# Two edits to a graph and expert network: the bases load into runs of 30 partitions, and slots are looked up by one-hot products inside the routed stage

## The chip, the cores and the metric

The kernel runs on one core of a Trainium2 chip. Its time is the device time of one execution in microseconds (us); of several executions the median is given. A profile shows one execution: its span runs from the first instruction to the last.

## The reference, cut to what matters

A network over 10,000 nodes of width 512: a relational graph network, a feed-forward layer with 16 experts, a four-layer graph network and a quantized feed-forward layer. Two pieces of it are touched. The relation weights are sums over 30 bases:

```python
w = jnp.einsum('rb,bio->rio', att, basis)        # basis (30, 512, 512), att (2, 30), for each of two layers
```

and in the expert layer each expert takes the 625 tokens with the largest probability for it:

```python
flat_probs = probs.transpose(2, 0, 1).reshape(En, T)      # (16, 10000)
scores, tok_idx = jax.lax.top_k(flat_probs, cap)          # cap = 625
toks = xf[tok_idx]
h = jax.nn.gelu(jnp.einsum('ecd,edh->ech', toks, w1) + b1[:, None, :])
y = jnp.einsum('ech,ehd->ecd', h, w2) + b2[:, None, :]
y = y * scores[..., None]
routed = jnp.zeros_like(xf).at[tok_idx.reshape(-1)].add(y.reshape(-1, Dn))
```

A token may be taken by several experts, so the sums of different experts meet in the same rows. Within one expert all tokens differ.

## The kernel before, in words

The program is a row of stages (`core.phase`), each with its own semaphores and ended by a barrier of all engines. In a stage every engine has its own instruction list, written out by hand: `pipeline` and `static_pipeline` take a list of (lag, step) and issue, turn by turn, step(turn - lag) in the order of the list. `pipeline` rolls the middle turns into a loop, `static_pipeline` writes all out.

`front_phase` sorts the edges, normalizes the rows of x and combines the bases. The 512 input rows of a basis matrix are taken in blocks of 64 (`SIDE`); a product on PE (line 558) has contraction 120 = 30 bases x 4 rows (`BASIS_ROWS`), and its stationary operand `spread` holds the att values in a staircase, so that 16 products give 64 rows of both relations. SP loads half a block as four transfers, one for each `quarter` (line 353), into `ba_t`: partition 4b + quarter holds basis b. One transfer fills 30 partitions, each with 8 rows of 2 KB, and the 30 source places lie 1 MiB apart. `spread` is filled in the same order (line 342). Four halves fit into the ring; SP waits for `cb` before it reuses one. Between the bases stand the loads of x (line 358), and stores of `normed` and of the combined blocks go out on ACT's queue.

The expert layer: `tokens_phase` writes the probabilities. `select_phase` finds each expert's 625 largest and leaves in DRAM `table`, for each expert 80 rows (`NB`), one for each block of 125 tokens (`BLOCK`), with the running rank and the score of each token, and `ends`, the rank at each block's end. The 625 slots of an expert are five tiles (`TPE`) of 125 partitions (`SL`).

`slots_phase` turns slots into tokens. It loads `ends` into all 125 partitions (line 1408), counts for each slot the blocks that end before it (lines 1430, 1433), and gathers the slot's table row with one indirect DMA per tile, 80 in all (line 1418). Two passes over the row (lines 1447, 1449) count the token's place and pick its score.

`routed_phase` then works expert by expert. POOL gathers five tiles of rows (line 1521), PE transposes them (`turn_slots`, line 1543), ACT and DVE split them into a high part (`high`, line 1581) and a low part (`low`, line 1616), `up` multiplies by w1 (24 products), ACT applies gelu and takes the high part (lines 1586, 1589), DVE the low one (`low_units`, line 1629), `down` multiplies by w2, `weigh` scales by the score into `res[i]` (line 1624), and POOL adds `res[i]` into the DRAM rows with an accumulating scatter (line 1529). POOL's order is: scatters of expert e - 3, gathers of expert e. A scatter batch waits until all scatters of the expert before it have landed. There is one `res` tile for each i, and `weigh(i)` waits until the scatter that read it has landed; on DVE `low(i)` and `weigh(i)` alternate. `norm_phase` follows; its first instruction is SP's load at line 1650.

`three` (lines 684 to 686) issues a product as three, high x high, low x high and high x low.

## Time and profile before

| | us |
|---|---|
| median of 3 executions | 5510.89 (5507.32 to 5512.34) |
| the profiled execution | 5506.21 |
| its span | 5504.4 |
| PE busy | 4216.8 (77%) |
| DVE busy | 2992.2 (54%) |
| ACT busy | 2139.4 (39%) |
| POOL busy | 1455.9 (26%) |

The stages stand one behind the other, so a time within the span names a stage: the front stage lies before 460 us, the slots stage from 2031 to 2180, the routed stage from 2180 to 2576. Busy shares over the whole span mix stages with different limits; the stage's own rows say what it waits for. The DMA share is the mean busy share of the 16 DMA engines. "issue" names idle time that no semaphore explains.

### The profile page before, as it was taken

The page shows a single profiled execution, that of the slowest core. Times are in us where ns is not written, and L with a number is a line of the kernel's source. Part 1 is how long each engine was busy: PE and PEld are TensorE (multiplying, and loading weights), DVE is VectorE, ACT ScalarE, POOL GpSimd, SP SyncE. Part 2 cuts the span into 40 slices and gives each one's busy share as a digit, 9 for nine tenths or more (in the row PEclk, how much of TensorE's full clock was granted, in tenths as well). Part 3 has the DMA queues.
Part 4 walks back from the last instruction along what each step waited for, and adds up shares of the span by engine and source line. Part 5 has one row for each costly group of instructions (what it writes and reads, how often), then busy time and mean ns, then how long its engine had stood idle before and what let it go on. Part 6 is the DMA issues. An engine that isn't in the chain of part 4 may idle for free. (4 is left out here: it accounts for less than half of the span.)

```text
span 5504.4 us, 70253 instructions
## 1 busy us (share of the span) xinstructions
PE 4216.8 (77%) x22571; PEld 3378.6 (61%) x22571; DVE 2992.2 (54%) x6700; ACT 2139.4 (39%) x3450; POOL 1455.9 (26%) x1380
## 2 busy tenths in 40 slices
PE   5766989799897710663389897989889897989533
PEld 2334868688786610542179773988579774988311
DVE  3435754377685564434755445554455435554588
ACT  0111213222337800220133564347533664347566
POOL 1322112211340007774433004310233004310243
PEclk9887999899998855665589995999789995999755
DMA  8994237722896603666955226532555127532354
GB/s 235 295 273 152 77 114 250 238 72 71 330 401 244 235 20 90 121 127 157 330 177 162 76 94 231 162 112 91 194 171 162 72 96 234 162 106 92 136 195 161
DMA packets 493679, 924.32 MB, mean 168 GB/s; under 512 B 107759, under 2 KB 108039, under 8 KB 492632
## 3 DMA queue, kind: packets, MB, share of 16 engines
q1 hardware_dynamic: 296076, 532.11, 29.2%
q0 software_dynamic: 118272, 237.34, 15.8%
q10 hardware_dynamic: 79088, 151.77, 7.6%
q8 instruction: 136, 2.23, 0.2%
q14 instruction: 107, 0.88, 0.0%
HBM read 597.24 MB, written 322.46 MB: 167 GB/s over the span
## 5 line engine op out<-in xcount | busy, mean ns | idle before, releaser
L684 PE MATMUL hidden_O<-hidden_xh,w_hi 128*128 128x256 f32 (+1 forms) x2560 | 728.8, 285 | 0.3 <-DVE hidden_xl L1057 0.2
L685 PE MATMUL hidden_O<-hidden_xh,w_lo 128*128 128x256 f32 (+1 forms) x2560 | 717.0, 280 | 0.0
L686 PE MATMUL hidden_O<-hidden_xl,w_hi 128*128 128x256 f32 (+1 forms) x2560 | 716.8, 280 | 0.0
L684 PE MATMUL output_O<-w_hi,output_hh 128*128 128x512 f32 (+1 forms) x1264 | 503.3, 398 | 56.5 <-DVE output_hl L1950 56.5
L1829 POOL DMA_INDIRECT hidden_agg<-edge_sums,edge_where x316 | 339.6, 1075 | 756.8 <-DVE hidden_xin L1876 605.6
L1860 ACT ACTIVATE hT<-hidden_O,hidden_b 128x256 f32<-128x256 f32 (+1 forms) x640 | 247.6, 469 | 659.1 <-PE hidden_O L686 659.1
L685 PE MATMUL output_O<-w_hi,output_hl 128*128 128x512 f32 (+1 forms) x1264 | 502.4, 397 | 0.0
L686 PE MATMUL output_O<-w_lo,output_hh 128*128 128x512 f32 (+1 forms) x1264 | 502.1, 397 | 0.0
L684 PEld LDWEIGHTS hidden_O<-hidden_xh,w_hi 128*128 128x128 f32 x2560 | 484.4, 189 | 1.5 <-DVE hidden_xl L1057 1.4
L685 PEld LDWEIGHTS hidden_O<-hidden_xh,w_lo 128*128 128x128 f32 x2560 | 485.2, 190 | 0.0
L686 PEld LDWEIGHTS hidden_O<-hidden_xl,w_hi 128*128 128x128 f32 x2560 | 483.3, 189 | 0.0
L1956 DVE TENSOR_TENSOR output_y<-output_O,output_b2t 128x1024 f32<-128x1024 f32 (+1 forms) x160 | 193.7, 1211 | 510.9 <-PE output_O L686 510.9
L1882 DVE BATCH_NORM_STATS2 h_stats<-hT 128x6 f32<-128x256 f32 (+1 forms) x640 | 221.1, 408 | 447.0 <-ACT hT L1860 447.0
L1732 POOL DMA_INDIRECT message_x<-g,edge_partner x160 | 174.5, 1091 | 821.8 <-issue 722.0
L558 PE MATMUL order_cb_ps<-order_basis,order_spread 120*128 120x512 f32 x512 | 269.2, 680 | 79.1 <-DMA order_basis<-in_L_gnn_basis 79.1
L1966 ACT ACTIVATE hT<-hT,output_shf,output_scl (+2 forms) x640 | 326.7, 581 | 0.0
L684 PEld LDWEIGHTS output_O<-w_hi,output_hh 128*128 128x128 f32 (+1 forms) x1264 | 237.6, 188 | 116.1 <-issue 56.7
L686 PEld LDWEIGHTS output_O<-w_lo,output_hh 128*128 128x128 f32 (+1 forms) x1264 | 237.4, 188 | 60.3
L685 PEld LDWEIGHTS output_O<-w_hi,output_hl 128*128 128x128 f32 (+1 forms) x1264 | 237.7, 188 | 59.8
L1774 PE MATMUL message_X<-message_attr_terms,message_edge_terms 5*128 5x512 f32 x160 | 125.1, 787 | 186.8 <-DMA message_attr_terms<-edge_attr_rows 183.2
L684 PE MATMUL root_O<-root_hi,root_xh 128*128 128x512 f32 (+1 forms) x632 | 254.1, 402 | 0.0
L684 PE MATMUL relation_B<-w_hi,relation_pth 128*128 128x512 f32 x640 | 253.6, 396 | 0.0
(376 smaller groups left out, 10014.4 us busy)
## 6 DMA issues: line engine op xcount, KB each, us to landing
hidden_xin<-g SPq DMA_DIRECT2D x156, 512.0 KB, 4.0
g<-output_y SPq DMA_DIRECT2D x156, 512.0 KB, 2.7
order_basis<-in_L_gnn_basis SPq DMA_DIRECT2D x128, 480.0 KB, 16.5
edge_sums<-message_res SPq DMA_DIRECT2D x160, 256.0 KB
edge_sums<-relation_res SPq DMA_DIRECT2D x80, 256.0 KB, 2.0
order_x<-in_x SPq DMA_DIRECT2D x39, 512.0 KB, 17.9
normed<-order_y ACTq DMA_DIRECT2D x39, 512.0 KB, 9.2
root_xin<-normed SPq DMA_DIRECT2D x39, 512.0 KB, 3.7
```

The costliest lines, as they stand in the source:

```text
L558: m = eng.matmul(cb_ps[j % 2][:, :], spread[n][:, at:at + P], ba_t[(2 * j + half) % W][:, k % HALF, :], start=k == 0, stop=k == SHARE - 1)
L684: eng.matmul(out, a_hi, b_hi, start=start, stop=False)
L685: eng.matmul(out, a_lo, b_hi, start=False, stop=False)
L686: return eng.matmul(out, a_hi, b_lo, start=False, stop=stop)
L1732: eng.indirect_dma_start(x[t % R][:, :], None, table, bass.IndirectOffsetOnAxis(ap=ed.partner[1][:, t:t + 1], axis=0)).then_inc(ga[t % R], 16)
L1774: eng.matmul(X[t % 2][:, :], edge_terms[:, t * P:(t + 1) * P], attr_terms[:, :], start=True, stop=True).then_inc(s["E"], 1)
L1829: eng.indirect_dma_start(agg[j % R][0:n, :], None, ed.sums[1], bass.IndirectOffsetOnAxis(ap=ed.where[1][0:n, c:c + 1], axis=0)).then_inc(g ...
L1860: m = eng.activation(hT[:, o, at(g)], O[g % 2][:, o, 0:width_of(last(g))], ACT.Identity, bias=b1t[:, o:o + 1])
L1882: m = eng.bn_stats(stats[:, o, g, :], hT[:, o, at(g)])
L1956: eng.tensor_tensor(part(y[q], last), part(O[q], last), b2t[0:n, :].unsqueeze(1).to_broadcast([n, k, D]), ALU.add).then_inc(s["add"], 1)
L1966: m = eng.activation(hT[:, o, at(g, w_)], hT[:, o, at(g, w_)], ACT.Relu, bias=shf[:, o:o + 1], scale=scl[:, o:o + 1])
```

## The change

In `front_phase` the partition of basis b and row quarter becomes 30 x quarter + b, in `ba_t` and in `spread`; nothing else there changes.

`slots_phase` is removed. `routed_phase` loads the whole table with block rows on 80 partitions (`lines`), the ends of the blocks (`end`) and, shifted by one partition, their beginnings (`begin`). For each expert DVE builds `hot`, an 80 x 625 matrix that is 1 where a slot's rank falls into a block (`place`), PE multiplies it with the expert's table rows, which puts each slot's row on its partition (`look`), ACT copies the result out of PSUM (`copy_lines`), and DVE does the two passes of before and adds the block's first token (`find`). The stage is written out in full. Gathers keep three x buffers in place of two, `res` has two sets of five tiles in place of one, `T` and `O` have two PSUM buffers each in place of three, and the gathers of an expert wait for one semaphore for all five tiles. POOL's order stays: scatters of an expert, then the gathers of the one two further on.

```diff
-                            eng.dma_start(spread[n][quarter:BASIS_ROWS:4, at:at + 1], att[r].rearrange("(b one) -> b one", one=1),
+                            eng.dma_start(spread[n][quarter * BASES:(quarter + 1) * BASES, at:at + 1], att[r].rearrange("(b one) -> b one", one=1),
                                           allow_slow_non_contiguous=True).then_inc(s[f"att{n}"], 16)
                 for k in range(KEYS):
...
                     for quarter in range(4):
-                        eng.dma_start(ba_t[i % W][quarter:BASIS_ROWS:4, :, :], src_[:, quarter, half * HALF:(half + 1) * HALF, :]).then_inc(ba[i % W], 16)
+                        eng.dma_start(ba_t[i % W][quarter * BASES:(quarter + 1) * BASES, :, :], src_[:, quarter, half * HALF:(half + 1) * HALF, :]).then_inc(ba[i % W], 16)
...
-def slots_phase(core, table, ends, token, score):
...
+def routed_phase(core, cst, rows_in, w1, b1, w2, b2, table, ends, routed):
...
+        lines = sbuf("lines", [NB, EXPERTS, WIDE])
+        end, begin = sbuf("end", [NB, EXPERTS]), sbuf("begin", [NB, EXPERTS])
+        base = sbuf("base", [NB, EXPERTS])
+        order = sbuf("order", [NB, CAP])
+        r0, r1 = sbuf("r0", [SL, TPE]), sbuf("r1", [SL, TPE])
+        past, hot = ring("past", [NB, CAP]), ring("hot", [NB, CAP])
+        junk, found, line = ring("junk", [SL, 2, BLOCK]), ring("found", [SL, 1]), ring("line", [SL, WIDE])
+        token, score = sbuf("token", [SL, ST], U32), sbuf("score", [SL, ST])
...
+        x = ring("x", [SL, TPE, D], ways=R)
...
+        res = [ring(f"res{i}_", [SL, D]) for i in range(TPE)]
+        T = [psum(f"T{j}", [P, KC, P]) for j in range(2)]
+        L = [psum(f"L{j}", [SL, 512]) for j in range(2)]
...
+                eng.dma_start(end[:, :], ends.rearrange("(e b) -> b e", b=NB), allow_slow_non_contiguous=True).then_inc(s["ends"], 16)
+                eng.wait_ge(s["first"], 1)
+                eng.dma_start(begin[1:NB, :], ends.rearrange("(e b) -> b e", b=NB)[0:NB - 1, :], allow_slow_non_contiguous=True).then_inc(s["ends"], 16)
+                for e in range(EXPERTS):
+                    eng.dma_start(lines[:, e, 0:2 * BLOCK], table[e * NB:(e + 1) * NB, :]).then_inc(s["tab"], 16)
+                for e in range(EXPERTS):
+                    q = e % 2
+                    wait(eng, s["wlo"], (e - 1) * 2)
+                    wait(eng, s["act"], e - 1)
+                    eng.dma_start(w1r[q][:, :, :], chunked(w1[e])).then_inc(wt[q], 16)
+                    eng.dma_start(w2r[q][0:HID, :], w2[e]).then_inc(wt[q], 16)
+                    eng.dma_start(w2r[q][HID:K, :], b2[e].unsqueeze(0)).then_inc(wt[q], 16)
+                    eng.dma_start(b1r[q][:, :], b1[e].unsqueeze(1)).then_inc(wt[q], 16)
...
+                def gather(e):
+                    eng.wait_ge(s["tok"], (e + 1) * TPE)
+                    wait(eng, s["T"], (e - R + 1) * TPE)
+                    for i in span:
+                        n = e * TPE + i
+                        eng.indirect_dma_start(x[e % R][:, i, :], None, rows_in,
+                                               bass.IndirectOffsetOnAxis(ap=token[:, n:n + 1], axis=0)).then_inc(ga[e % R], 16)
+
+                def scatter(e):
+                    wait(eng, s["sws"], e * LAND)
+                    for i in span:
+                        n = e * TPE + i
+                        eng.wait_ge(s["ev"], n + 1)
+                        eng.indirect_dma_start(routed, bass.IndirectOffsetOnAxis(ap=token[:, n:n + 1], axis=0), res[i][e % 2][:, :], None,
+                                               compute_op=ALU.add).then_inc(s["sws"], 16)
+                static_pipeline([(3, scatter), (1, gather)], EXPERTS)
+                eng.wait_ge(s["sws"], EXPERTS * LAND)
...
+                def look(e):
+                    eng.wait_ge(s["hot"], 2 * e + 2)
+                    for i in span:
                         n = e * TPE + i
...
+                        wait(eng, s["line"], n - 1)
+                        eng.matmul(L[n % 2][:, 0:WIDE], hot[e % 2][:, i * SL:(i + 1) * SL], lines[:, e, :], start=True, stop=True).then_inc(s["look"], 1)
...
+                for r in range(EXPERTS + 3):
+                    if r < EXPERTS:
+                        look(r)
+                    turn_and_down(r)
+                    if 0 <= r - 2 < EXPERTS:
+                        up(r - 2)
...
+                def copy_lines(e):
+                    for i in span:
+                        n = e * TPE + i
+                        eng.wait_ge(s["look"], n + 1)
+                        wait(eng, s["tok"], n - 1)
+                        eng.activation(line[n % 2][:, :], L[n % 2][:, 0:WIDE], ACT.Copy).then_inc(s["line"], 1)
...
+                static_pipeline([(0, copy_lines), (2, high), (2, acts), (1, weights)], EXPERTS)
...
+                def place(e):
+                    q = e % 2
+                    wait(eng, s["look"], (e - 1) * TPE)
+                    eng.tensor_scalar(past[q][:, :], order[:, :], begin[:, e:e + 1], None, ALU.is_ge).then_inc(s["hot"], 1)
+                    eng.wait_ge(s["hot"], 2 * e + 1)
+                    eng.scalar_tensor_tensor(hot[q][:, :], order[:, :], end[:, e:e + 1], past[q][:, :], ALU.is_lt, ALU.mult).then_inc(s["hot"], 1)
+
+                def find(e):
+                    for i in span:
+                        n = e * TPE + i
+                        own = line[n % 2]
+                        eng.wait_ge(s["line"], n + 1)
+                        eng.tensor_scalar(junk[n % 2][:, 0, :], own[:, 0:BLOCK], r0[:, i:i + 1], 0.0, ALU.is_le, ALU.add,
+                                          accum_out=found[n % 2][:, :]).then_inc(s["cnt"], 1)
+                        eng.scalar_tensor_tensor(junk[n % 2][:, 1, :], own[:, 0:BLOCK], r1[:, i:i + 1], own[:, BLOCK:2 * BLOCK],
+                                                 ALU.is_equal, ALU.mult, accum_out=score[:, n:n + 1])
+                        eng.wait_ge(s["cnt"], n + 1)
+                        eng.tensor_tensor(token[:, n:n + 1], found[n % 2][:, :], own[:, 2 * BLOCK:WIDE], ALU.add).then_inc(s["tok"], 1)
...
+                def low_and_weigh(r):
+                    e, f = r - 2, r - 3
+                    for i in span:
+                        if 0 <= e < EXPERTS:
+                            n = e * TPE + i
+                            cols = slice(i * SL, (i + 1) * SL)
+                            eng.wait_ge(s["hi"], n + 1)
+                            eng.tensor_tensor(xl[e % 2][:, :, cols], T[n % 2][:, :, 0:SL], xh[e % 2][:, :, cols].bitcast(F32),
+                                              ALU.subtract).then_inc(s["lo"], 1)
+                        if 0 <= f < EXPERTS:
+                            n = f * TPE + i
+                            wait(eng, s["sws"], (f - 1) * LAND)
+                            eng.wait_ge(s["O"], n + 1)
+                            eng.tensor_scalar(res[i][f % 2][:, :], O[n % 2][:, :], score[:, n:n + 1], None, ALU.mult).then_inc(s["ev"], 1)
...
+                eng.wait_ge(s["ends"], 32)
+                place(0)
+                for r in range(EXPERTS + 3):
+                    if r < EXPERTS:
+                        find(r)
+                    if r + 1 < EXPERTS:
+                        place(r + 1)
+                    low_and_weigh(r)
+                    if 0 <= r - 1 < EXPERTS:
+                        weights(r - 1)
+                    if 0 <= r - 2 < EXPERTS:
+                        low_units(r - 2)
```

On SP, between the select stage and the first weight load, one load of `slots_end` gives way to 18 loads:

```order
 L1297 DMA slot_ends<-select_last 128x10
 L1288 UNCONDITIONAL_BRANCH
-L1406 UNCONDITIONAL_BRANCH
-L1408 DMA slots_end<-slot_ends 125x1280
-L1405 UNCONDITIONAL_BRANCH
-L1503 UNCONDITIONAL_BRANCH
-L1509 DMA routed_w1r<-in_L_ffn_w 128x4x64
```

```order
+L1420 UNCONDITIONAL_BRANCH
+L1422 DMA routed_end<-slot_ends 80x16x1
+L1424 DMA routed_begin<-slot_ends 79x16x1
+L1426 DMA routed_lines<-slot_table 80x250 x16
+L1431 DMA routed_w1r<-in_L_ffn_w 128x4x64
```

The first weight load moved behind all of them. On DVE, in the middle of the routed stage, from one expert's `low_units` to the next expert's first `low` and `weigh`, stands before:

```order
L1629 TENSOR_TENSOR routed_gl<-routed_act,routed_gh 65x628
L1608 TENSOR_TENSOR routed_w1l<-routed_w1r,routed_w1h 128x256
L1610 TENSOR_TENSOR routed_w2l<-routed_w2r,routed_w2h 65x512
L1603 COPY routed_sc<-slot_score 125x5
L1604 COPY routed_ix<-slot_token 125x5
L1616 TENSOR_TENSOR routed_xl<-routed_T,routed_xh 128x4x125
L1624 TENSOR_SCALAR routed_res<-routed_O,routed_sc 125x512
```

and now (the first three of these rows come five times, once for each tile):

```order
L1559 TENSOR_SCALAR routed_junk,routed_found<-routed_line,routed_r 125x125
L1561 SCALAR_TENSOR_TENSOR routed_junk,routed_score<-routed_line,routed_r 125x125
L1564 TENSOR_TENSOR routed_token<-routed_found,routed_line 125x1
L1550 TENSOR_SCALAR routed_past<-routed_order,routed_begin 80x625
L1552 SCALAR_TENSOR_TENSOR routed_hot<-routed_order,routed_end,routed_past 80x625
L1580 TENSOR_TENSOR routed_xl<-routed_T,routed_xh 128x4x125
L1586 TENSOR_SCALAR routed_res_0<-routed_O,routed_score 125x512
```

The lookups of an expert and the placement of the next stand between the splits of an expert's units and the first `low` of the next turn. On POOL the order of the fused stage begins:

```order
L1448 DMA routed_x<-normed,routed_token 125x512 x10
L1456 DMA x<-routed_res_0,routed_token 10000x512 x5
L1448 DMA routed_x<-normed,routed_token 125x512 x5
L1456 DMA x<-routed_res_1,routed_token 10000x512 x5
L1448 DMA routed_x<-normed,routed_token 125x512 x5
```

Ten gathers stand ahead of the first scatters, where 15 stood before; after that five and five alternate in both.

## Rows read from the trace of the kernel before

**Rows 1.** Windows, front stage: us; PE, PEld, DVE, ACT, POOL busy; clock; DMA share; GB/s.

```profile
46.00:60.00 14.00, 14.00 (x28) 5.89 (x27) 0.00 (x0) 0.00 (x0) 0.00 (x0) 1.00 0.99 218
100.00:350.00 250.00, 189.78 (x543) 90.55 (x541) 108.73 (x471) 45.45 (x62) 79.38 (x108) 0.86 1.01 297
```

**Rows 2.** DMA issues, page: count, size of one, us from issue to landing.

```profile
order_basis<-in_L_gnn_basis SPq DMA_DIRECT2D x128, 480.0 KB, 16.5
```

**Rows 3.** Groups of instructions, whole span: busy us, mean ns; idle us before, and releaser.

```profile
L558 PE MATMUL order_cb_ps<-order_basis,order_spread 120*128 120x512 f32 x512 | 269.2, 680 | 79.1 <-DMA order_basis<-in_L_gnn_basis 79.1
...
L1418 POOL DMA_INDIRECT slots_line<-slot_table,slots_ix x80 | 97.8, 1223 | 44.3 <-DVE slots_ix L1442 22.8 <-issue 16.3 <-DVE slots_junk L1449 5.2
...
L1624 DVE TENSOR_SCALAR routed_res<-routed_O,routed_sc 125x512 f32<-125x512 f32 x80 | 60.0, 750 | 134.8 <-issue 75.2 <-DMA x<-routed_res,routed_ix 54.1 <-PE routed_O L686 5.3
...
L1616 DVE TENSOR_TENSOR routed_xl<-routed_T,routed_xh 128x500 fp32r<-128x500 f32 x80 | 53.6, 670 | 9.8 <-ACT routed_xh L1581 9.8
```

**Rows 4.** Windows (columns as in Rows 1) of the routed stage and of slots_end's load.

```profile
2180.00:2576.00 396.00, 237.76 (x944) 185.13 (x944) 138.85 (x241) 84.60 (x149) 261.04 (x160) 0.63 0.63 115
2034.00:2035.00 1.00, 0.00 (x0) 0.00 (x0) 0.00 (x0) 0.00 (x0) 0.00 (x0) 0.50 0.31 128
```

**Rows 5.** Timeline, start of the slots stage: start us, us, engine, line, what.

```profile
2032.19 0.28 SPq L1408 DMA_DIRECT2D slots_end<-slot_ends  x1
...
2039.85 4.07 DVE L1430 TENSOR_SCALAR slots_cmp<-slots_end,slots_r 125x1280 f32<-125x1280 f32 x5 [6.40 <-DMA slots_end<-slot_ends]
...
2055.80 0.35 DVE L1447 TENSOR_SCALAR_CACHE_REDUCE slots_junk<-slots_line,slots_r 125x125 f32<-125x125 f32 x1 [4.26 <-DMA slots_line<-slot_table,slots_ix]
...
2056.07 0.35 DVE L1449 SCALAR_TENSOR_TENSOR slots_junk<-slots_line,slots_r 125x125 f32<-125x125 f32 x1
...
2056.34 0.15 DVE L1442 COPY slots_ix<-slots_row 125x1 uint32<-125x1 uint32 x1
```

**Rows 6.** Timeline of POOL in the routed stage, and SP's first issue after it.

```profile
2181.28 1.21 POOL L1521 DMA_INDIRECT routed_x<-normed,routed_ix  x1 [6.29 <-DVE routed_ix L1604]
...
2214.68 2.05 POOL L1529 DMA_INDIRECT x<-routed_res,routed_ix  x1 [0.30 <-issue]
...
2327.29 2.01 POOL L1529 DMA_INDIRECT x<-routed_res,routed_ix  x1 [4.02 <-DVE routed_res L1624]
...
2336.93 1.98 POOL L1529 DMA_INDIRECT x<-routed_res,routed_ix  x1 [0.30 <-issue]
...
2348.73 2.02 POOL L1529 DMA_INDIRECT x<-routed_res,routed_ix  x1 [2.17 <-DVE routed_res L1624]
...
2550.79 1.98 POOL L1529 DMA_INDIRECT x<-routed_res,routed_ix  x1 [9.94 <-DVE routed_res L1624]
...
2576.02 1.93 SPq L1650 DMA_DIRECT2D norm_x<-x  x4
```

**Rows 7.** Timeline of PE, ACT and DVE in one expert's period of the routed stage.

```profile
2323.79 0.49 PE L684 MATMUL routed_Hp<-routed_xh,routed_w1h 128*64 128x314 f32 x1 [3.72 <-DVE routed_xl L1616]
...
2329.20 0.78 ACT L1586 ACTIVATE routed_act<-routed_Hp,routed_b1r 64x628 f32<-64x628 f32 x1 [9.78 <-PE routed_Hp L686]
...
2330.65 0.40 ACT L1574 ACTIVATE routed_w1h<-routed_w1r 128x256 fp32r<-128x256 f32 x1
...
2347.70 0.75 DVE L1624 TENSOR_SCALAR routed_res<-routed_O,routed_sc 125x512 f32<-125x512 f32 x1 [0.57 <-issue]
```

**Rows 8.** Timeline of SP in the relation stage: loads into 64 partitions each.

```profile
464.64 10.36 SPq L743 DMA_DIRECT2D w_hi<-combined1hi  x16
```

**Rows 9.** DMA view, 2792 to 2793 us (hidden_b, 512 elements): packets and queues.

```profile
DMA packets 572, 0.09 MB, mean 90 GB/s; under 512 B 546, under 2 KB 546, under 8 KB 572
...
q1 hardware_dynamic: 555, 0.02, 44.0%
```

**Rows 10.** Windows (columns as in Rows 1) while those 64-partition loads run.

```profile
474.00:484.00 10.00, 0.00 (x0) 0.00 (x0) 0.36 (x3) 0.14 (x1) 1.94 (x2) 0.50 1.04 276
```

**Rows 11.** Page, section 2: GB/s of the core's DMA in 40 slices of the span.

```profile
GB/s 235 295 273 152 77 114 250 238 72 71 330 401 244 235 20 90 121 127 157 330 177 162 76 94 231 162 112 91 194 171 162 72 96 234 162 106 92 136 195 161
```

222 lines of the change are left out of this document (53 added, 169 removed).

## The prediction

> **What bounds the kernel now.** The one core runs stages one after another, each ended by a barrier, so a stage's saving is the program's. I cut the span by stage first; the change touches two places.
>
> *Front stage* (0 to 460 us). From 46 to 60 us the queue holds only bases: 218 GB/s at a DMA share of 0.99. From 100 to 350 us, with x loads and stores between them, 297 GB/s at 1.01, PE busy 190 of 250 us [rows 1]. All DMA engines are taken all the time and PE has a quarter to spare: DMA sets this stage. The 128 transfers of 480 KiB [rows 2] are 62.9 MB, 289 us at 218 GB/s, so what they cost per byte matters most. PE's 512 products (680 ns, 79.1 us of waiting for bases) [rows 3] follow.
>
> *Slots stage* (2031 to 2180 us). No PE and no ACT work; GpSimd issues 80 gathers of one table row per slot, 1.2 us each with 0.3 between, 121 of the 149 us; before them lie a broadcast load and ten wide DVE passes [rows 3, 4, 5].
>
> *Routed stage* (2180 to 2576 us). First scatter 2214.68, sixteenth batch 2550.79: 336.1 us for 15 experts, 22.4 each [rows 6]. PE is busy 238 of 396 us at a mean clock of 0.63 [rows 4], so it is not full. The batches must not overlap, since they add into shared rows. In one batch the fifth scatter goes out 9.64 us after the first (2327.29, 2336.93), the DVE product that waits for it starts at 2347.70, so it landed in 10.8, and the next batch starts 1.0 later, at 2348.73 [rows 6, 7]: 21.4 us. That loop, not an engine, sets the pace. The missing 1.0 us on average comes from `res`: with one set of five tiles DVE stands in `weigh` for a landing, and the next expert's `low` queues behind it, then `up` on PE.
>
> **The change, part by part.**
>
> 1. *The slots stage goes.* The stretch from SP's first issue at 2032.19 to the first routed gather at 2181.28 [rows 5, 6], 149.1 us, is replaced by items 2 and 3.
>
> 2. *Start of the fused stage.* Two element-wise loads of the block ends, 1,280 and 1,264 elements of 4 bytes, stand ahead of the first DVE placement, on SP before 16 table loads (at the 0.65 us an issue of [rows 8], 10 us). A 512-element load on all engines elsewhere: 546 small packets in one us, at 44% of 16 engines (with some larger ones), so 13 ns busy and 29 ns elapsed per packet and engine [rows 9]. But engines are shared out by partition count: the 125-partition load `slots_end` ran at a share of 0.31, five of sixteen [rows 4]. 125 is 25 times 5; 79 has no divisor, so I take one engine for `begin`: 1,264 packets at 13 to 29 ns, 16 to 37 us. Nothing covers it: `place(0)` waits for it, and lookup, gathers and PE wait for `place(0)`. Bounds for that moment: 2042 (all engines) and 2072; I take 2060, 25 us of load, inside one engine's two prices.
> The Trainium skill, DMA: Bandwidth & Descriptors, section on why a DMA increments its semaphore by 16, gives the rule: the largest number up to 16 that divides both sides' slowest dimension. The trace agrees for 125 (0.31 x 16 = 5.0); by the rule 79 gives 1.
>
> 3. *Filling the pipeline.* A lookup of a tile is two DVE passes (0.54 us from start to start) and one narrow one (0.15) [rows 5], with waits 0.75; its PE product is fp32 over 251 columns, half of a 680 ns row [rows 3], its ACT copy 0.40 [rows 7]: with two buffers 0.9 a tile, 5 an expert. Placement is two passes over 625 columns: 0.4 (half of a 1,280-wide pass, 0.81) and 0.84 (from 500 columns, 0.67) [rows 3, 5], 1.3. Three experts are looked up before the first transposes: 19 us, which hides the first gathers. Then five tiles 7, `up` 6, gelu and splits 4, lookup and placement 5, first product 2: first scatter 43 us after `place(0)`, at 2103. Bounds 38 and 50.
>
> 4. *The pace.* POOL's order is as before (five scatters, five gathers); their own time, 19 us an expert, and landings stay. `res` gets two sets, so a landing no longer holds `low`. Scatter loop: 21.4, as worked out above; I take 21.0 as its low bound. The engine loop gets longer: from the end of `up`, ACT 2.4 (gelu, high parts, weights) and DVE's rest to 3.8 us [rows 7], five lookups 3.8, placement 1.3, five pairs of `low` and `weigh` 7.1 [rows 3], one to two us more since two PSUM buffers (three before) make PE wait for DVE, `up` 5.4 (2323.79 to 2329.20) [rows 7]: 22 to 23 at most, 20 if PE keeps the higher clock. PE gains under 3 us an expert on 14. Two loops about equal, no longer chained: 22.0, bounds 21.0 and 24.0. Cover for the lookup is thus the scatter landing; if it goes, the engine loop is the pace.
>
> 5. *Tail.* From the sixteenth batch's first scatter to norm_x's load: 25.2 us (2550.79 to 2576.02) [rows 6], kept.
>
> 6. *Bases in runs of 30.* Same bytes, packets, issues and products; only which partitions a transfer fills. Strided, alone: 218 GB/s at 0.99. The nearest row of the new kind, 128 KiB loads into 64 neighbouring partitions, moves 276 at 1.04 [rows 8, 10]. So neither form has an edge that I can name; between 218 kept and 276 I take zero, because both are engines waiting on something shared at full share, and the source rows (1 MiB apart) do not change. Bounds: gain 62.9 MB at 276, 228 us, so 61 less; loss 20, if mixing with x stops helping (with the x loads and stores 2.6 MB a turn: 1.4 MB at 218 and the rest at 401, the best slice of the page [rows 11], takes 9.4 us, not 8.9 as now at 297; 40 turns).
> The Trainium skill, SBUF — State Buffer, section Door 1: The DMA port swizzle, speaks against the edit: bandwidth goes with how many of 16 ports a transfer's partitions reach, and 32 neighbours reach eight, half of 128. By it the old form, spread over 120 partitions, should near 436 GB/s and the new one 218. The trace differs on the old form: it already moves only 218.
>
> **Sum.** 2060 + 43 + 15 x 22.0 + 25.2 = 2458 against 2576: 118 us less. The profiled execution took 5506.2 (span 5504.4): 5388. The median shown, 5510.9, is 5 above; I leave that inside the range. Bounds of the routed part: 2042 + 38 + 315 + 25 = 2420 (156 less) to 2072 + 50 + 360 + 25 = 2507 (69 less).
>
> **Rivals.**
> - *A. Bases get faster.* Neighbouring partitions reach the 276 of [rows 10]: 30 to 61 less again, 5327 to 5358. For: the row. Against: other source, 64 partitions. 0.13.
> - *B. The engine loop takes over.* DVE's order puts five lookups and a placement between `low_units` and the next `low`; PE idles meanwhile, falls to the lower clock, and the period is 25 to 27: 45 to 75 more, 5433 to 5463. For: 22 to 23 is already near. Against: DVE is under 70% busy. 0.14.
> - *C. One-engine load.* 80 to 100 ns an element instead of 20: 75 to 100 more, 5463 to 5488. Against: [rows 9]. 0.07.
> - *D. Slower than before.* Each transfer now fills a narrow band, and engines queue at it: half the places, 109 GB/s, 577 us instead of 289, PE waiting for bases throughout: 5388 + 289 = 5677. It decides below 155 GB/s (62.9 MB in 289 + 118 us). Against: 276 into 64 neighbours; for: the page above, whose halving it is, started from the measured 218. 0.06.
>
> The rest, 0.60, is the forecast.
>
> **Numbers.** A measurement of this kernel tells 0.2%, 11 us, from no change. Forecast, A, B and C are faster, D slower, as are a few mixtures: faster 0.91, same 0.02, slower 0.07. The forecast's own bounds together would be 5327 to 5457; with A's near end and most of B inside, and C and D out, 5340 to 5445 holds about 0.8.
>
> **What would show it.** Slots stage absent; `place(0)` near 2060 with one engine's share of DMA before it; first scatter near 2103; batches 21.4 to 22.5 apart, POOL's wait before them shorter or on DMA landings; norm_x's load near 2458. Bases alone 210 to 230 GB/s, front stage ending within 20 us of now. Wrong if: the gap before `place(0)` exceeds 45 us (C); batches are over 24 apart with `res` ready late (B); the GB/s of the bases alone leaves 200 to 240 (A, D).

## Result and profile after

The changed kernel takes 5548.2 us against 5509.1: a ratio of 1.0075, 95% interval 1.0059 to 1.0091. It is slower by some 39 us where 118 less were forecast, outside the stated range. The profiled execution spans 5547.6 us.

| stretch (us) | forecast | before | after |
|---|---|---|---|
| front stage, up to SP's first load of the relation stage | no change | 463.3 | 510.7 |
| from there to SP's first load of the block ends | no change | 1568.9 | 1571.1 |
| block ends' load to the first placement | 28 | | 9.4 |
| first placement to the first scatter | 43 | | 49.5 |
| 15 periods of the batches | 330 (22.0 each) | 336.1 (22.4) | 451.4 (30.1) |
| sixteenth batch to norm_x's load | 25.2 | 25.2 | 25.1 |
| block ends' load to norm_x's load | 426 | 543.8 | 535.5 |
| norm_x's load to the end | no change | 2928.4 | 2930.3 |

Two things went wrong: the front stage lost 47.4 us, and the fused stage, 118 shorter by the forecast, is only 8 shorter, because each batch takes 8 us more than forecast. With the 2 us of the stretch between and the 2 behind, 47.4 + 2.2 - 8.3 + 1.9 are the 43.2 by which the spans differ.

The windows of the changed kernel, columns as in [rows 1] and answering to [rows 1, 4]; the third is the 15 periods, the last the time in which the load of the block begins runs:

```profile
46.00:60.00 14.00, 12.95 (x80) 7.17 (x79) 0.00 (x0) 0.60 (x1) 0.00 (x0) 1.00 1.01 194
100.00:350.00 250.00, 174.72 (x486) 83.41 (x487) 99.79 (x434) 41.81 (x57) 73.63 (x100) 0.85 1.01 266
2141.00:2592.00 451.00, 275.38 (x999) 210.40 (x997) 184.83 (x516) 97.06 (x191) 238.41 (x145) 0.61 0.53 91
2084.00:2090.00 6.00, 0.00 (x0) 0.00 (x0) 0.00 (x0) 0.00 (x0) 0.00 (x0) 0.50 0.10 1
```

The bases alone move 194 GB/s (218 before), in the mix 266 (297), at the same full DMA share. A 2 KiB packet thus holds an engine longer: 0.99 of 16 engines for 14 us over some 1,490 big packets were 149 ns each, 1.01 over 1,325 are 171. For the same bytes 266 GB/s take 12% longer than 297; over some 400 us of the front stage that is, as an estimate, the 47 us. In the routed stage DMA (0.53), PE (275 of 451 us), DVE and POOL all have room: nothing is full, so a ring of waits, each engine waiting for the next and the last for the first, sets the pace. The group of PE's basis products answers to [rows 3]:

```profile
L558 PE MATMUL order_cb_ps<-order_basis,order_spread 120*128 120x512 f32 x512 | 278.6, 698 | 93.5 <-DMA order_basis<-in_L_gnn_basis 93.5
```

Its wait for bases rose from 79.1 to 93.5 us. The ring shows in the timelines of one period. POOL of the changed kernel:

```profile
2327.43 2.02 POOL L1456 DMA_INDIRECT x<-routed_res,routed_token  x1 [11.71 <-DVE routed_res L1586]
2329.76 2.00 POOL L1456 DMA_INDIRECT x<-routed_res,routed_token  x1 [0.30 <-issue]
...
2336.62 1.99 POOL L1456 DMA_INDIRECT x<-routed_res,routed_token  x1 [0.30 <-issue]
2338.91 1.26 POOL L1448 DMA_INDIRECT routed_x<-normed,routed_token  x1 [0.30 <-issue]
...
2345.38 1.23 POOL L1448 DMA_INDIRECT routed_x<-normed,routed_token  x1 [0.31 <-issue]
2357.61 2.02 POOL L1456 DMA_INDIRECT x<-routed_res,routed_token  x1 [10.99 <-DVE routed_res L1586]
```

PE, from its last lookup products to the next expert's first transposes:

```profile
2344.33 1.20 PE L1468 MATMUL routed_L<-routed_lines,routed_hot 80*125 80x251 f32 x2 [1.15 <-ACT routed_line L1522]
2353.44 1.10 PE L1478 MATMUL routed_T<-cst_ident,routed_x 125*128 125x125 f32 x4 [7.91 <-DMA routed_x<-normed,routed_token]
```

DVE, from the placement to the first pass on those transposes:

```profile
2347.16 0.87 DVE L1552 SCALAR_TENSOR_TENSOR routed_hot<-routed_order,routed_end,routed_past 80x625 f32<-80x625 f32 x1
2355.26 0.68 DVE L1580 TENSOR_TENSOR routed_xl<-routed_T,routed_xh 128x500 fp32r<-128x500 f32 x1 [7.23 <-ACT routed_xh L1529]
```

The reader is to follow it once around. The first scatter goes out at 2327.43; five of them, then the first gather at 2338.91 (11.5 later); the fifth gather at 2345.38; PE, idle for 7.91 us, starts the transposes at 2353.44, 8.1 after the fifth gather's issue, inside the 5.1 to 10.7 us in which gathers land in the kernel before (view below); DVE's split and weighing follow, and the next first scatter goes out at 2357.61 (4.2 later). 11.5 + 14.5 + 4.2 = 30.2 us, the period. POOL waits 10.99 us for a product that waits for what POOL issued last. The gathers' landing in the kernel before, least, median and longest:

```profile
DMA to landing us min/median/max: 5.1/8.3/10.7
```

The chief waits of the 15 periods (sum, times, longest) say the same:

```profile
POOL x L1456 <- DVE routed_res L1586: 184.4, 16, 20.3
...
PE routed_T L1478 <- DMA routed_x<-normed,routed_token: 135.4, 14, 15.0
```

In the kernel before, the gathers of expert e follow the scatters of e - 3 on POOL, and their rows are transposed beside the product of e - 1. The scatters of e - 2 still lie between these gathers and the scatters of e - 1, so the rows have a whole turn to land. Since a lookup now takes a turn, the gathers of e follow the scatters of e - 2 and are due beside the product of e - 1, the very next to be scattered. The order shown ahead of the prediction, ten gathers before the first scatters where 15 stood, is that lost turn; the sentence there that POOL's order stays is wrong in this. A second part of the ring is the wait ahead of the transposes of line 1478: it is for all five gathers of the expert, where before each tile had a semaphore of its own.

The start of the fused stage, all engines:

```profile
2081.82 0.34 SPq L1422 DMA_DIRECT2D routed_end<-slot_ends  x1
...
2082.22 0.49 SPq L1424 DMA_DIRECT2D routed_begin<-slot_ends  x1
...
2082.75 14.57 SPq L1426 DMA_DIRECT2D routed_lines<-slot_table  x16
...
2091.26 0.55 DVE L1550 TENSOR_SCALAR routed_past<-routed_order,routed_begin 80x625 f32<-80x625 f32 x1 [8.27 <-DMA routed_begin<-slot_ends]
...
2098.84 4.55 PE L1468 MATMUL routed_L<-routed_lines,routed_hot 80*125 80x251 f32 x10 [26.74 <-DMA routed_lines<-slot_table]
...
2140.78 2.04 POOL L1456 DMA_INDIRECT x<-routed_res,routed_token  x1 [20.28 <-DVE routed_res L1586]
```

The sixteen table loads, one by one (ns, least, median and longest):

```profile
L1426 SPq DMA_DIRECT2D routed_lines<-slot_table x16: 422/425/7566, 2082.8 to 2096.9; - x16
```

Fifteen took SP 0.42 us each. The first, right behind the long load of `routed_begin`, held SP for 7.57 us, and of data only 4-byte packets moved meanwhile: the tables did not load beside it but after it.

### The profile page after: what moved, and what is told of

Read it like the earlier page. It is cut to its first block and busy times, and to the rows that moved or that the text cites. A ratio compares the mean times of both kernels' runs of the same rounds, so it can differ in the third digit from the quotient of the medians.

```text
span 5547.6 us, 69307 instructions
## 1 busy us (share of the span) xinstructions
PE 4301.2 (78%) x22731; PEld 3432.0 (62%) x22731; DVE 2993.5 (54%) x6606; ACT 2169.7 (39%) x3530; POOL 1360.8 (25%) x1302
## 5 line engine op out<-in xcount | busy, mean ns | idle before, releaser
L1931 DVE TENSOR_TENSOR output_y<-output_O,output_b2t 128x1024 f32<-128x1024 f32 (+1 forms) x160 | 193.8, 1212 | 512.0 <-PE output_O L686 512.0
L558 PE MATMUL order_cb_ps<-order_basis,order_spread 120*128 120x512 f32 x512 | 278.6, 698 | 93.5 <-DMA order_basis<-in_L_gnn_basis 93.5
L558 PEld LDWEIGHTS order_cb_ps<-order_basis,order_spread 120*128 120x128 f32 x512 | 111.8, 228 | 229.4 <-issue 125.3
## 6 DMA issues: line engine op xcount, KB each, us to landing
hidden_xin<-g SPq DMA_DIRECT2D x156, 512.0 KB
g<-output_y SPq DMA_DIRECT2D x156, 512.0 KB
order_x<-in_x SPq DMA_DIRECT2D x39, 512.0 KB
normed<-order_y ACTq DMA_DIRECT2D x39, 512.0 KB
root_xin<-normed SPq DMA_DIRECT2D x39, 512.0 KB
```

The source lines that it names most:

```text
L558: m = eng.matmul(cb_ps[j % 2][:, :], spread[n][:, at:at + P], ba_t[(2 * j + half) % W][:, k % HALF, :], start=k == 0, stop=k == SHARE - 1)
L1931: eng.tensor_tensor(part(y[q], last), part(O[q], last), b2t[0:n, :].unsqueeze(1).to_broadcast([n, k, D]), ALU.add).then_inc(s["add"], 1)
```

## Experiments

All are compared with the kernel before in the same set of runs. "Alone" is the window from 46 to 60 us, "mixed" 100 to 350. Eight kernels here keep every fourth partition and the old source and show how far such windows differ from one execution to another: 215 to 227 alone, 297 to 308 mixed, relation stage's first load at 453.9 to 463.3.

### The two parts apart

`runs_only`: the kernel before, with

```diff
-spread[n][quarter:BASIS_ROWS:4, at:at + 1]
+spread[n][quarter * BASES:(quarter + 1) * BASES, at:at + 1]
-ba_t[i % W][quarter:BASIS_ROWS:4, :, :]
+ba_t[i % W][quarter * BASES:(quarter + 1) * BASES, :, :]
```

> The kernel before with the bases in runs of 30 partitions and nothing else. Theory: the new form itself slows the transfers (149 ns a packet and engine before, 171 in the changed kernel), so the front stage ends 45 to 50 us later and the program takes 5509 + 47 = 5556 us; the bases alone move 190 to 200 GB/s. Rival: the partitions are innocent and something else of the changed kernel (other allocations, other addresses) shifted the front stage: 5509 and 218 GB/s.

5561.5 us, ratio 1.0091 (1.0075 to 1.0106): 47 us, as expected. The relation stage's first load comes at 504.9, 42 us later than before; the profiled execution was the shortest of four, 5542.9. Its windows:

```profile
46.00:60.00 14.00, 13.34 (x83) 7.42 (x82) 0.00 (x0) 0.60 (x1) 0.00 (x0) 1.00 1.01 195
100.00:350.00 250.00, 175.38 (x498) 83.85 (x498) 100.59 (x436) 43.32 (x59) 73.64 (x100) 0.86 1.01 267
```

`stage_only`: the changed kernel with the opposite edit.

> The changed kernel with the bases back in every fourth partition. Theory: the two parts add up, so this one takes 5548 - 47 = 5501 us, 8 less than before: slots and routed stage together 535 us against 544, batches still 30 us apart. Rival: slow transfers ahead shift something later too, and the routed stage gets better by itself: under 5490.

5493.3 us, ratio 0.9973 (0.9959 to 0.9987): some 15 us below before, 7 to 23 by the interval; from block ends to norm_x 527.4 us, period 29.6. The expected 8 lie inside the interval, and the ring is there without the bases edit. The two parts, +47 and -7 to -23, make up the whole, 39, within that interval. Its windows:

```profile
46.00:60.00 14.00, 14.00 (x28) 5.90 (x28) 0.00 (x0) 0.00 (x0) 0.00 (x0) 1.00 0.99 220
100.00:350.00 250.00, 187.99 (x551) 91.93 (x550) 112.59 (x488) 47.21 (x65) 82.39 (x112) 0.87 1.01 303
```

### What sets the period of the batches

`gather_early`: stage_only with

```diff
-static_pipeline([(3, scatter), (1, gather)], EXPERTS)
+static_pipeline([(3, scatter), (0, gather)], EXPERTS)
```

> stage_only with each expert's gathers issued one turn earlier (15 ahead of the first scatters, as before, in place of 10). Theory: the period is the ring scatters (11.5) - gathers - landing of the last of five (14.5 from the first issue) - transpose, product, weigh (4.2), 30.2 in all, since the gathers for the very next transposes stand behind the scatters. With the gathers a turn ahead PE no longer waits for them; the next limits are the engines' own ring, about 23, and the scatter ring, 21.4: period 22.5 to 24, 15 x 6.5 = 98 us less than stage_only, about 5403. Rival (the lookups on DVE, PE and ACT stretch the engines' ring): the period stays at 29 to 30, 5495 to 5505.

5378.0 us, ratio 0.9765 (0.9749 to 0.9782), 115 us below stage_only, where 98 were expected: the period is 21.95 us ((2418.02 - 2088.72) / 15), a little under the expected 22.5 to 24. POOL in one period, and PE at its change from lookups to transposes:

```profile
2178.04 2.02 POOL L1456 DMA_INDIRECT x<-routed_res,routed_token  x1 [2.42 <-DMA x<-routed_res,routed_token]
...
2189.53 1.26 POOL L1448 DMA_INDIRECT routed_x<-normed,routed_token  x1 [0.30 <-issue]
...
2195.68 1.23 POOL L1448 DMA_INDIRECT routed_x<-normed,routed_token  x1 [0.31 <-issue]
2201.01 2.01 POOL L1456 DMA_INDIRECT x<-routed_res,routed_token  x1 [4.10 <-DMA x<-routed_res,routed_token]
```

```profile
2193.87 1.11 PE L1468 MATMUL routed_L<-routed_lines,routed_hot 80*125 80x251 f32 x2 [1.15 <-ACT routed_line L1522]
2194.77 1.04 PE L1478 MATMUL routed_T<-cst_ident,routed_x 125*128 125x125 f32 x4
```

Here the first scatter of the next batch waits for a landing (4.10 us, DMA), and PE goes from lookup products to transposes without any wait. So it is in nine of the 15 batches behind the first; in the other six the first scatter still waits for the DVE product, as in this one, the landing being 1.3 to 2.4 us past by then:

```profile
2244.40 2.02 POOL L1456 DMA_INDIRECT x<-routed_res,routed_token  x1 [2.72 <-DVE routed_res L1586]
```

Scatter ring and engines' ring are thus about equally long here. The lost turn was worth 7.6 us an expert, and with it restored the pace is what the prediction had forecast.

`tile_semaphores`: stage_only with

```diff
-eng.indirect_dma_start(...).then_inc(ga[e % R], 16)
+eng.indirect_dma_start(...).then_inc(ga[e % 2 * TPE + i], 16)
-eng.wait_ge(ga[e % R], (e // R + 1) * LAND)
+eng.wait_ge(ga[e % 2 * TPE + i], (e // 2 + 1) * 16)
```

> stage_only with a semaphore for each tile's gather, so that a tile's transposes wait for their own gather and not for all five. Same order of everything. Theory: the first transposes start at the first landing, 6 us (four gathers of 1.52) sooner; the others come every 1.5 us, faster than the engines take them (2.1): period 24 to 25, 80 to 90 us less than stage_only, about 5415. Rival (the engines' ring with its lookups is what ends the period): within 15 us of stage_only.

5446.1 us, ratio 0.9882 (0.9867 to 0.9897), 47 below stage_only, where 80 to 90 were expected; period 26.3. Right in kind, too large in size: POOL's first gather, PE's transposes behind it, and the next first scatter:

```profile
2288.76 1.26 POOL L1449 DMA_INDIRECT routed_x<-normed,routed_token  x1 [0.30 <-issue]
...
2300.55 0.70 PEld L1479 LDWEIGHTS routed_T<-cst_ident,routed_x 125*128 125x128 f32 x4 [5.69 <-DMA routed_x<-normed,routed_token]
...
2304.71 2.02 POOL L1457 DMA_INDIRECT x<-routed_res,routed_token  x1 [8.59 <-DVE routed_res L1587]
```

The transposes start 11.8 us after their own gather's issue; the expectation took the first gather to land as fast as the fifth, in 8.1. The kernel before had shown this: of the gathers that follow scatters the first of five lands 10.3 us after its issue (median of 13 experts), the fifth 7.1, so the 8.3 of all gathers is no figure for the first. That the scatters' packets ahead of it in the queue cause this fits, but was not tried. So the ring is 3.3 us shorter, not 6.

`lookups_threefold`: stage_only with two further pairs of lookup passes a tile on DVE.

```diff
+for more in range(2):
+    eng.tensor_scalar(spare[n % 2][:, 2 * more, :], own[:, 0:BLOCK], r0[:, i:i + 1], 0.0, ALU.is_le, ALU.add)
+    eng.scalar_tensor_tensor(spare[n % 2][:, 2 * more + 1, :], own[:, 0:BLOCK], r1[:, i:i + 1], own[:, BLOCK:2 * BLOCK], ALU.is_equal, ALU.mult)
```

> stage_only with each tile's two lookup passes on DVE done three times (two further pairs into spare tiles, 5.4 us more DVE work an expert; the results are not used). Theory (the ring of scatters, gathers and transposes ends the period and DVE stands idle 7 us before each expert's first product): period stays 29.5 to 30.5, the time within 15 us of stage_only, about 5495. Rival (the lookups in DVE's order are what stretched the period from 22 to 30): 5 us more an expert, about 5575.

One run, 5519.1; period 30.3 us against 29.6. Of the added 5.4 us of DVE an expert 0.7 shows, so lookups did not stretch the period from 22 to 30. The time is still above what was expected: the first scatter comes 75 us after the block ends' load, not 60, since at the start nothing covers them.

`early_lookups_threefold`: gather_early with the same edit.

> gather_early with the same threefold lookups. There two rings are about equal at 22.0 (scatters and landing; the engines, with the lookups in it), so nothing covers the additional 5.4 us: period 26 to 28, 15 x 5 = 75 us more than gather_early, about 5450. Rival (the scatters' landing alone ends the period and DVE has slack): under 5395.

One run, 5441.9, 64 us above gather_early; mean period 24.6. Both readings missed, the first narrowly, and the mean mixes two parts. As long as lookups go on, in the first twelve periods, it is 25.6 ((2415.39 - 2108.36) / 12) against gather_early's 22.3 ((2356.81 - 2088.72) / 12), and all twelve first scatters waited for the DVE product; the last three, without lookups, waited for landings. So the engines' ring set the pace here, and 3.3 of the added 5.4 us show in it. Where the other 2.1 went was not followed.

`early_one_res`: gather_early with one set of result tiles.

```diff
-wait(eng, s["sws"], (f - 1) * LAND)
+wait(eng, s["sws"], f * LAND)
-eng.tensor_scalar(res[i][f % 2][:, :], O[n % 2][:, :], score[:, n:n + 1], None, ALU.mult)
+eng.tensor_scalar(res[i][0][:, :], O[n % 2][:, :], score[:, n:n + 1], None, ALU.mult)
```

(and the scatters read that set)

> gather_early with one set of result tiles instead of two, so that DVE's weighing of an expert waits until the scatters of the expert before have landed, as in the kernel before. Theory (item 4 of the prediction: with two sets the landing no longer holds DVE's order): the wait puts scatter ring and engines' ring in a chain; period 23 to 24.5, 15 to 35 us more than gather_early, about 5400. Rival (two sets are of no use, since the scatters wait for the same landings anyway): period 22, 5378.

5404.2 us, ratio 0.9789 (0.9773 to 0.9806) against 0.9765; the intervals overlap, so this rests on the traces. The period is 23.1 ((2440.08 - 2093.11) / 15), and from block ends to norm_x pass 431.3 us instead of 414.7. The second set is worth about 1.2 us an expert, near the 1.0 of the prediction and the low end of what was expected here.

### The start of the fused stage

`early_begin_spread`: gather_early with

```diff
-eng.dma_start(begin[1:NB, :], ends.rearrange("(e b) -> b e", b=NB)[0:NB - 1, :])
+eng.dma_start(begin[1:NB, 0:1], ends[0:NB - 1].rearrange("(b e) -> b e", e=1))
+eng.dma_start(begin[:, 1:EXPERTS], ends[NB - 1:EXPERTS * NB - 1].rearrange("(e b) -> b e", b=NB))
```

and row 0 cleared afterwards.

> gather_early with the block begins loaded so that all engines share it: columns 1 to 15 into 80 partitions, the first column apart (79 elements), row 0 cleared after them. Theory: the load of 79 partitions ran on one engine, 9.0 us from issue to the first placement; now 2.5 to 3.5 us, first scatter 5 to 6 us sooner, all of it on the path: about 6 us less than gather_early, ratio to before 0.9755. Rival (the 16 table loads behind it or the weights set the start, not this load): no change.

5379.1 us, ratio 0.9746 (0.9731 to 0.9762); the intervals of 0.9746 and 0.9765 overlap, so this rests on the trace: block ends' load to first placement 4.0 us instead of 9.6, to norm_x's load 407.7 instead of 414.7. No table load holds SP any more (0.69 us at most, against 7.57 for the first in the changed kernel), and the first lookup product starts 10.9 us after the block ends' load instead of 17.3. In the timeline, the last row is the first placement:

```profile
2034.90 0.34 SPq L1422 DMA_DIRECT2D routed_end<-slot_ends  x1
...
2035.30 0.49 SPq L1424 DMA_DIRECT2D routed_begin<-slot_ends  x1
...
2035.84 0.63 SPq L1425 DMA_DIRECT2D routed_begin<-slot_ends  x1
...
2038.94 0.54 DVE L1552 TENSOR_SCALAR routed_past<-routed_order,routed_begin 80x625 f32<-80x625 f32 x1
```

### Why runs of 30 are slower

The first guess was the span of a transfer's partitions, that is, how far apart they lie. In all nine forms of this section the source of a transfer is read at 30 places 1 MiB apart, and that was not changed; what holds every fourth partition at 220 GB/s is therefore open. `bases_stride2`: stage_only with

```diff
-ba_t[i % W][quarter:BASIS_ROWS:4, :, :]
+ba_t[i % W][60 * (quarter // 2) + quarter % 2:60 * (quarter // 2) + 60:2, :, :]
```

(the spread weights' rows likewise)

> stage_only with the bases in every second partition of one half (0 to 59 or 60 to 119) instead of every fourth of 120. Theory (what a transfer's packets cost grows as its partitions crowd together): alone between the 218 to 220 GB/s of stride four and the 194 of runs, 203 to 213, and a front stage 15 to 30 us longer than stage_only's, about 5518. Rival 1 (only directly neighbouring partitions, which one engine fills one after the other, cost more): like stride four, 218 to 220, 5495. Rival 2 (any narrower band costs in full): 194, 5542.

5526.9 us, ratio 1.0035 (1.0022 to 1.0047):

```profile
46.00:60.00 14.00, 13.45 (x26) 5.60 (x26) 0.00 (x0) 0.00 (x0) 0.00 (x0) 1.00 0.98 193
100.00:350.00 250.00, 187.77 (x529) 89.07 (x528) 105.87 (x457) 46.97 (x64) 77.24 (x106) 0.87 1.00 292
```

Alone it is like runs (rival 2), mixed nearer to every fourth partition, and in the time between the two, as the theory had it.

`bases_all120`: stage_only with

```diff
-for quarter in range(4):
-    eng.dma_start(ba_t[i % W][quarter:BASIS_ROWS:4, :, :], src_[:, quarter, half * HALF:(half + 1) * HALF, :])
+for k in range(HALF):
+    eng.dma_start(ba_t[i % W][0:BASIS_ROWS, k, :], src_[:, :, half * HALF + k, :])
```

> stage_only with each half block of bases moved by eight transfers of 120 partitions (one for each k, 2 KiB a partition, its source 8 KiB in a row) in place of four of 30. Same bytes and 2 KiB packets, twice the issues on SP. Theory (spread over all 120 partitions is what counts, and 4 neighbours lie in one engine's share): if neighbours in one engine's share cost, as in runs, 190 to 200 GB/s and some 45 us more than stage_only, about 5540; if only the span of a whole transfer counts, 215 GB/s or more and 5495 or less. The second is the theory's own value if bases_stride2 lands in between; a longer contiguous source could add to it.

5467.8 us, ratio 0.9927 (0.9906 to 0.9949), 25 us below stage_only and faster than every fourth partition:

```profile
46.00:60.00 14.00, 14.00 (x41) 6.29 (x41) 0.00 (x0) 0.38 (x1) 0.00 (x0) 1.00 1.00 242
100.00:350.00 250.00, 193.06 (x582) 93.84 (x580) 116.25 (x505) 50.61 (x69) 87.33 (x118) 0.89 1.00 314
```

`source_in_a_row`: stage_only with

```diff
-rearrange("b (j k q) o -> j b q k o", j=BLOCKS, q=4)[b]
+rearrange("b (j q k) o -> j b q k o", j=BLOCKS, q=4)[b]
-at = SIDE - 4 + r * SIDE + quarter
+at = SIDE - 4 + r * SIDE + quarter * SHARE
-at = SIDE - 4 - 4 * k
+at = SIDE - 4 - k
```

> stage_only (bases in every fourth partition) with the four row groups of a block of bases taken as 16 neighbouring rows each, in place of every fourth row, so that a partition's 16 KiB are one piece of the source; the spread weights and the products' column offsets are moved to match, the destination partitions are the same. Theory (where a transfer lands sets its speed, as runs_only, bases_stride2 and bases_all120 order themselves by how far a transfer's partitions are spread: 195, 193, 219, 242 GB/s): within 15 us of stage_only, 215 to 225 GB/s alone, about 5495. Rival (bases_all120 was faster for its 8 KiB of source in a row): 240 GB/s or more, 30 us or more less than stage_only, 5465 or less.

5473.0 us, ratio 0.9908 (0.9893 to 0.9923). Alone 228, little more than stride four's 215 to 227; mixed 323, and the front stage 21 us shorter than stage_only's, by the ratios 36 us in all. Neither reading came true: the rate alone is the theory's, the time nearer to the rival's. So a source in a row, with packets of 16 KiB, helps in the mix.

`source_row_one_load`: the four transfers of 30 partitions joined to one of 120.

```diff
-for quarter in range(4):
-    eng.dma_start(ba_t[i % W][quarter:BASIS_ROWS:4, :, :], src_[:, quarter, half * HALF:(half + 1) * HALF, :])
+eng.dma_start(ba_t[i % W].ap().rearrange("p k o -> p (k o)"), src_[:, :, half * HALF:(half + 1) * HALF, :].rearrange("b q k o -> b q (k o)"))
```

> As source_in_a_row, and the four transfers of 30 partitions joined to one of all 120, 1.9 MiB: each engine then fills 8 neighbouring partitions, as in bases_all120. Theory of the spread: 240 GB/s or more whatever source_in_a_row does, some 30 us less than stage_only, about 5463. If the source counted, both are fast and this one adds nothing: within 8 us of source_in_a_row.

5548.9 us, ratio 1.0054 (1.0038 to 1.0069), front stage as long as with runs, though each transfer spans all 120 partitions. The theory of the span falls here:

```profile
46.00:60.00 14.00, 13.35 (x27) 5.45 (x26) 0.00 (x0) 0.00 (x0) 0.00 (x0) 1.00 0.95 202
100.00:350.00 250.00, 178.13 (x502) 85.40 (x503) 100.45 (x436) 41.27 (x57) 73.57 (x100) 0.84 0.97 268
```

What does put the rates alone in order is how many bytes an engine writes before it leaves a group of four neighbouring partitions. This assumes that fifteen engines share a transfer, each with neighbouring partitions as its share; no run shows the shares. It gives 8 KiB in bases_all120, 16 with every fourth partition, 64 in one load. Three kernels tried that.

`row_runs`: the changed kernel (destination in runs) with source_in_a_row's source.

> The changed kernel (bases in runs of 30 partitions) with the source of source_in_a_row. Only the destination differs from source_in_a_row, and only the source from the changed kernel. Theory (runs of 30 cost by the destination alone): 190 to 200 GB/s alone, front stage 45 to 60 us longer than in source_in_a_row, time like the changed kernel's less at most 15, about 5540. Rival (the runs hurt only with 2 KiB pieces of source, by more, smaller packets): 225 GB/s, 5475.

5543.9 us, ratio 1.0047 (1.0021 to 1.0073), relation stage's first load at 512.0: with the better source runs are as slow as ever (204 alone, 262 mixed). It differs from source_in_a_row in the destination alone, so it is the destination that makes runs slow.

`row_120_by_1`: bases_all120's destination with source_in_a_row's source.

> bases_all120 with the rows of source_in_a_row: eight transfers of 120 partitions, the destination exactly that of bases_all120, but each partition's 2 KiB from a place of its own in the source in place of 8 KiB in a row for four. Theory (what counts is how soon an engine moves from one group of four partitions to the next: after 8 KiB here and in bases_all120, 242; 16 KiB with stride four, 219 and 228; 64 KiB in source_row_one_load, 202; never in runs, 194): 235 to 250 GB/s alone, and the time of bases_all120, ratio 0.993. Rival (bases_all120 was fast for its source): 220 GB/s or less, ratio 0.997 or more.

5471.6 us, ratio 0.9932 (0.9916 to 0.9947), 276 alone, more than expected, 310 mixed. So bases_all120 owed its speed to how the destination is filled, not to 8 KiB of source in a row.

```profile
46.00:60.00 14.00, 14.00 (x40) 6.27 (x39) 0.00 (x0) 0.38 (x1) 0.00 (x0) 1.00 1.01 276
100.00:350.00 250.00, 193.67 (x573) 93.22 (x571) 116.14 (x505) 50.01 (x68) 85.98 (x117) 0.89 0.98 310
```

`row_120_by_2`: the same in four transfers of 4 KiB a partition (k in steps of 2).

> As row_120_by_1 with four transfers of 4 KiB a partition for each half block (an engine moves on after 16 KiB). Theory as there: between row_120_by_1 and source_row_one_load, near the values for 16 KiB, 215 to 230 GB/s, ratio 0.994 to 0.999. Rival (packets of 4 KiB instead of 2 count more, and the walk nothing): faster than row_120_by_1.

5480.3 us, ratio 0.9950 (0.9934 to 0.9965), 231 alone: between 276 and 202, at the value for 16 KiB. Between row_120_by_1, row_120_by_2 and source_row_one_load the size of packets and transfers grows with the walk, so these three by themselves do not tell the two apart; packets of one size, 2 KiB or 16, are in the table too.

| kernel | KiB in a group of four | packets | alone, mixed GB/s | relation stage's first load |
|---|---|---|---|---|
| row_120_by_1 | 8 | 2 KiB | 276, 310 | 430.1 |
| bases_all120 | 8 | 2 KiB | 242, 314 | 434.6 |
| source_in_a_row | 16 | 16 KiB | 228, 323 | 438.5 |
| row_120_by_2 | 16 | 4 KiB | 231, 311 | 449.7 |
| stage_only | 16 | 2 KiB | 220, 303 | 459.3 |
| runs_only | 32 | 2 KiB | 195, 267 | 504.9 |
| row_runs | 32 | 16 KiB | 204, 262 | 512.0 |
| bases_stride2 | 64 | 2 KiB | 193, 292 | 487.5 |
| source_row_one_load | 64 | 16 KiB | 202, 268 | 507.1 |

The Trainium skill, SBUF — State Buffer, section Door 1: The DMA port swizzle, says that four neighbouring partitions share a port, and partitions 32 apart too. By its table, as an estimate under the assumption above, fifteen engines in step with every fourth partition meet on eight ports and change to the other eight after 16 KiB; in runs of 30, where the next transfer goes 30 partitions on, they stay on nearly the same ones. The rates alone in the table above agree with that order: 276 and 242 with 8 KiB, 220 to 231 with 16, 193 to 204 with 32 and more. No run shows the ports themselves or why a sooner change should pay. In the mix the order does not hold: bases_stride2's 292, with 64 KiB, lies far above the 262 of row_runs with 32. So the destination's part is shown, the port as its mechanism is not.

### All that helped, together

`best`: stage_only with the edits of gather_early, early_begin_spread and bases_all120.

> The three edits that helped, together: gathers a turn earlier, the block begins loaded on all engines, and the bases in eight transfers of 120 partitions for each half block. They lie in stages behind barriers, so the savings add: 0.9765 for gather_early, 0.002 less for the begins, 0.005 to 0.006 less for the bases (bases_all120 0.9927 against stage_only 0.9973): ratio 0.969 to 0.971, about 5345. If a shorter front stage meets something else that ends it (PE, 190 of 250 us busy), less than 0.003 of it shows: 0.972 or more.

5356.9 us, ratio 0.9724 (0.9710 to 0.9737): 2.8% below before, 3.5% below the changed kernel (0.9724 / 1.0075). This is short of the expected 0.969 to 0.971; it lies where the other case was put, 0.972 or more, but PE as the end of the front stage does not show, since the relation stage's first load comes as early as in bases_all120. Its profiled span, 5344.2, is 27.5 us below gather_early's: the relation stage's first load comes at 433.7 instead of 455.3, and from there to the block ends' load pass 1567.5 us, as before, so nothing of that is taken back; block ends to norm_x take 412.0 instead of 414.7 (407.7 in early_begin_spread), the period being 22.3 here. Bases with the source in a row (ratio 0.9908 in source_in_a_row, against 0.9927 in bases_all120) were not put together with the other edits.

## Why the prediction was wrong, by its steps

- **Slots stage goes, 149.1 us.** Right; the stage is absent.
- **Start of the fused stage (item 2).** Mechanism right, price too high. From 2084 to 2090 us the DMA share is 0.10, one to two engines of sixteen; the 1,264 elements took 9.0 us from issue, where 16 to 37 was the estimate and 25 was taken. Packets of 4 bytes followed 5.9 ns apart here (1,020 in the 6 us), not 13 to 29: [rows 9] mixed them with larger ones. Spreading the load brought the first placement 5.6 us forward. The Trainium skill's rule for the share of engines, cited there, gives one engine for 79 partitions. The trace fits it, if packets overlap: each took 9.0 ns and the next started 5.9 later, which is the 0.10 x 16 = 1.6; one engine with overlap and two engines look the same in it.
- **Filling (item 3).** 49.5 instead of 43, inside the bounds. PE's first lookup product waited for the tables until 2098.84, 7.6 us after the placement: 16 loads took SP until 2097.32. The prediction had them hidden behind the long load (10 us of issues); the first of them held SP until that load was nearly done.
- **The pace (item 4) is the step that failed.** "POOL's order is as before (five scatters, five gathers); their own time, 19 us an expert, and landings stay." The order within a turn stayed; which expert's gathers stand in it did not. The prediction weighed two rings, scatters with landing and the engines, and never asked when the gathered rows are needed. Gathers a turn later, waited for all five at once, made a third: 30.1 us. That was none of the rivals: B gave 25 to 27 and for another cause, DVE's lookups, which the threefold lookups clear; the sign named for it, over 24 apart with `res` late, appeared all the same. With the turn restored the period is 21.95, so 22.0 was right for a kernel that the change isn't. Of its parts, the gain of a second `res` set is confirmed (1.2 us against 1.0), and so is "two loops about equal": with the turn restored nine of 15 batches waited for a landing and six for the engines' product.
- **Tail (item 5).** Right: 25.1.
- **Bases (item 6), the second step that failed.** Taken as zero with a loss of at most 20; measured 47, the form alone at 194 GB/s, outside the 200 to 240 that were to hold. The reasoning, "both are engines waiting on something shared at full share, and the source rows (1 MiB apart) do not change", was no bound on the destination's part. [Rows 10], 276 GB/s into 64 neighbours, spoke of another form. The direction was that of D, whose halving (109 GB/s) was far too much: 194. The Trainium skill's rule on ports, cited there, spoke against the edit rightly, with figures (436 and 218) that neither form reached. But the number of ports reached is not what decided: source_row_one_load fills all 120 partitions, which by that rule reach as many ports as every fourth of them, and moved 202.
- **Sum.** Restored to the measured values, 47.4 for the front and 8.1 x 15 = 121 for the pace, against 18.6 less for item 2 and 6.5 more for item 3, the forecast's 118 less turn into 39 more; with the 4 of the two stretches around the stage these are the 43 of the spans. One slip without effect: 5327, given as the low end of the forecast's own bounds together, counts the bases' gain alone (5388 - 61); with the routed part's 156 less as well it is 5289.

## What to carry to other kernels

When a change rewrites a software pipeline, write the turn of every step for one item, before and after, and walk each ring to its start: how long after a transfer is issued is it needed, and does its issue wait for what it feeds? A lag of one turn less in a queue that nobody had named as a bound cost 7.6 us an expert, more than all the arithmetic that was added. And put a price on where a transfer lands, not only on its bytes and packets: the same bytes moved at 202 to 276 GB/s with one source and at 193 to 242 with the other, by how the transfers fill the partitions.

## What the runs showed of the hardware

- The walk over destination partitions: 2 KiB packets at 276 or 242 GB/s with 8 KiB in a group of four, 220 with 16, 195 with 32 (which bytes an engine writes is assumed, see above); the DMA share is 0.99 to 1.01 in all of them, so it does not tell a fast form from a slow one.
- The first gather behind five scatters on POOL's queue was used 11.8 us after its issue in tile_semaphores and landed after 10.3 in the kernel before (median of 13), the fifth after 7.1; the median of all 8.3 hides the order.
- Element-wise 4-byte packets at a DMA share of 0.10, with no others running, followed each other every 5.9 ns, and the next load on the same queue held SP for 7.57 us instead of 0.42.
